# One sum tensor instead of two in a macaron block of two MoE layers and attention

## What is computed

```python
x = x + 0.5 * ffn(layernorm(x), w_gate, w_shared_up, w_shared_down, w_up, w_down)
x = x + attention(layernorm(x), Wq, bq, Wk, bk, Wv, bv, Wo, bo)   # 16 query heads, 1 key/value head of 32
x = x + 0.5 * ffn(layernorm(x), ...)

def ffn(x, ...):                       # E = 64 experts, top 6, room for CAP = 256 rows in each
    y_s, g_s = split(x @ w_shared_up)
    shared = silu(g_s) * y_s @ w_shared_down
    scores = sigmoid(x @ w_gate)
    w, topk_idx = top6(scores)         # w divided by its sum
    # pos = place of a row in its expert's list; rows beyond CAP are dropped
    x_disp[e, pos] = x[row]
    g_r, v_r = split(x_disp @ w_up)    # 512 -> 2 x 64, per expert
    out_r = silu(g_r) * v_r @ w_down   # 64 -> 512
    routed[row] = sum over the row's experts of w * out_r[e, pos]
    return shared + routed
```

## Time and profile before

| | us |
|---|---|
| median of 3 runs (lowest, highest) | 3214.35 (3210.79, 3216.09) |
| span of the profiled execution | 3211.7 |
| route0 | 0 to 185 |
| experts0 | 185 to 617 |
| project | 617 to 820 |
| attention | 820 to 2544 |
| route1 | 2544 to 2714 |
| experts1 | 2714 to 3143.5 |
| combine | 3143.5 to 3211.7 |

### The profile page before, as it was taken

One profiled execution on the slowest core, in us unless ns is written; L12 is line 12 of the kernel. 1 busy time (PEld: TensorE's weight loads), 2 busy tenths in 40 slices (PEclk: granted clock), 3 DMA queues, 4 the chain that ended last, 5 costly groups with the idle time before them and its releaser, 6 DMA issues. The chain is left out here.

```text
span 3211.7 us, 44845 instructions
## 1 busy us (share of the span) xinstructions
PE 2799.2 (87%) x15264; PEld 1631.1 (51%) x15264; DVE 2037.6 (63%) x3922; ACT 1526.7 (48%) x2871; POOL 2216.7 (69%) x1430
## 2 busy tenths in 40 slices
PE   8967777398899999999999999999999876888870
PEld 4644444176555555555555555555554374555540
DVE  7833222267788788788787887887876294333334
ACT  5522222153566566566565665665656352222220
POOL 2248888562688788788787887887878423677770
PEclk9978888699999999999999999999999867999995
DMA  5679999894567677676776776776757364899998
GB/s 213 214 203 241 246 235 235 198 276 168 118 146 145 132 171 146 147 148 140 154 150 132 172 142 147 147 145 149 155 121 153 104 212 154 202 233 234 243 184 321
DMA packets 216987, 575.78 MB, mean 179 GB/s; under 512 B 33980, under 2 KB 35004, under 8 KB 192824
## 3 DMA queue, kind: packets, MB, share of 16 engines
q0 software_dynamic: 87296, 343.98, 53.2%
q1 hardware_dynamic: 125240, 220.55, 21.1%
q10 hardware_dynamic: 4224, 8.39, 0.7%
HBM read 230.94 MB, written 155.24 MB: 120 GB/s over the span
## 5 line engine op out<-in xcount | busy, mean ns | idle before, releaser
L1915 DVE TENSOR_REDUCE attention_mx<-attention_pM 128x1 f32<-128x512 f32 x1984 | 1209.4, 682 | 180.1 <-PE attention_pM L1774 175.7
L1719 ACT ACTIVATE attention_prob<-attention_pS 128x512 f32<-128x512 f32 x2048 | 1035.9, 628 | 528.7 <-PE attention_pS L1761 528.5
L1660 POOL TENSOR_TENSOR attention_pair<-attention_prob 128x1024 f32<-128x1024 f32 x380 | 947.4, 2499 | 189.4 <-ACT attention_prob L1719 174.7
L1761 PE MATMUL attention_pS<-attention_qT,prep_kT 128*128 128x512 f32 x2048 | 832.7, 413 | 2.5 <-ACT attention_prob L1719 1.5
L1774 PE MATMUL attention_pM<-prep_kT,attention_qT 96*128 96x512 f32 x1984 | 804.4, 408 | 0.0
L1761 PEld LDWEIGHTS attention_pS<-attention_qT,prep_kT 128*128 128x128 f32 x2048 | 387.3, 189 | 289.4 <-issue 160.0
L1799 PE MATMUL attention_pO<-attention_prob,attention_v 128*32 128x512 f32 x4096 | 492.5, 598 | 0.0
L768 POOL DMA_INDIRECT sum<-experts_res,c_table x256 | 404.0, 1578 | 123.2 <-issue 78.0
L1774 PEld LDWEIGHTS attention_pM<-prep_kT,attention_qT 96*128 96x128 f32 x1984 | 374.7, 190 | 142.2 <-DVE attention_mx L1915 56.8
L752 POOL DMA_INDIRECT experts_rows<-xn_rows,c_table x256 | 250.7, 979 | 103.8 <-issue 71.3
L797 PE MATMUL experts_pT<-c_ident,experts_rows 128*128 128x128 f32 x1024 | 169.5, 306 | 120.2 <-issue 47.9
(11 more groups left out here) (181 smaller groups left out, 3141.3 us busy)
## 6 DMA issues: line engine op xcount, KB each, us to landing
prep_acc<-attention_pair POOLq DMA_DIRECT2D x96, 1024.0 KB, 7.7
attention_acc<-attention_pair POOLq DMA_DIRECT2D x90, 1024.0 KB, 7.6
attention_qT<-q_parts SPq DMA_DIRECT2D x96, 256.0 KB
xn_rows<-route_xn SPq DMA_DIRECT2D x16, 1152.0 KB, 6.7
experts_wup<-in_L_ffn_w_up_dram SPq DMA_DIRECT2D x64, 256.0 KB
q_parts<-prep_acc SPq DMA_DIRECT2D x64, 256.0 KB, 4.3
ahead_wup<-in_L_ffn_w_up_dram SPq DMA_DIRECT2D x64, 256.0 KB, 9.1
combine_got<-sum SPq DMA_DIRECT2D x16, 1024.0 KB
```

The source lines that it names most:

```text
L1660: pool.tensor_tensor(to[:, part], prob[2 * n % PROBS][:, part], prob[(2 * n + 1) % PROBS][:, part], ALU.add).then_inc(s_pair, 1)
L1719: act.activation(prob[t % PROBS][:, h * QT:(h + 1) * QT], pS[:, at, :], ACT.Exp).then_inc(s_ex, 1)
L1761: pe.matmul(pS[:, at, :], kT[:, key:key + P], qT[g][:, h, :], start=True, stop=True).then_inc(s_sc, 1)
L1915: dve.tensor_reduce(mx[:, unit, part:part + 1], pM[:, r % RING, :], X, ALU.max).then_inc(s_mr, 1)
```

## The change

Each FFN has one sum tensor. In the experts stage, both experts of a pair add onto it. The order on POOL becomes: two gathers, the two adds of a pair's first expert, two gathers, the two adds of its second one. The first two wait until the second expert's adds of the pair before have landed, the second two until the first two have. In `route0` POOL adds x to the shared rows (`with_x`), after `rsqrt` of the turn two ahead and ahead of the next `places`, and SP stores the result as the sum's start; x stays in its buffer until then, so that its ring has four buffers there, and a load waits for `with_x` too. `route1` writes no zeros, and the semaphore of the stored rows is split by ring slot. `project` loads one tensor, without `add_sums` and `bring`; `combine` loads one tensor and makes one addition a turn.

```diff
 def route(...)
-    XB, RING, HOTS = 3, 4, 2 * TURN
+    XB, RING, HOTS = 4 if kept is None else 3, 4, 2 * TURN
...
                 def load(i):
                     if i >= XB:
                         sp.wait_ge(s_xn, A + (i - XB + 1) * TURN)
+                        if kept is None:
+                            sp.wait_ge(s_sx, A + (i - XB + 1) * TURN)
...
-                    if copy_x:
-                        own_rows = slice(i * QT, (i + 1) * QT)
-                        sp.dma_start(sums[0][own_rows, :].rearrange("(p n) c -> p (n c)", p=P),
-                                     x_d[own_rows, :].rearrange("(p n) c -> p (n c)", p=P)).then_inc(s_nil, 16)
                     if kept is None:
-                        sp.wait_ge(s_sh, A + (i + 1) * TURN)
-                        sp.dma_start(half_view[i, :, :, :], sh[i % 2][:, :, :]).then_inc(s_so[i % 2], 16)
-                    else:
-                        sp.dma_start(half_view[i, :, :, :], zero[:, 0:C].unsqueeze(1).to_broadcast([P, TURN, C])
-                                     ).then_inc(s_so[i % 2], 16)
+                        sp.wait_ge(s_sx, A + (i + 1) * TURN)
+                        sp.dma_start(sum_view[i, :, :, :], sh[i % 2][:, :, :]).then_inc(s_so[i % 2], 16)
...
+                def with_x(i, j):
+                    pool.wait_ge(s_sh, A + i * TURN + (j + 1))
+                    pool.sem_inc(k["pool_on"], 1)
+                    pool.tensor_tensor(sh[i % 2][:, j, :], sh[i % 2][:, j, :], xt[i % XB][:, j, :], ALU.add
+                                       ).then_inc(s_sx, 1)
+
                 for i in range(-2, NTURN + 1):
...
+                    if comes(i) and kept is None:
+                        for j in range(TURN):
+                            with_x(i, j)
...
 def experts(...)
-                def add_rows(e):
-                    for a in range(2):
...
-                        if e > 0:
-                            pool.wait_ge(s_add[a], e * (16 * HALVES))
...
-                                sums[a], bass.IndirectOffsetOnAxis(ap=k["table"][:, 2 * e + a, h:h + 1], axis=0),
...
+                def add_rows(e, a):
...
+                    if a == 0 and e > 0:
+                        pool.wait_ge(s_add[1], e * (16 * HALVES))
+                        pool.sem_inc(k["pool_on"], 1)
+                    if a == 1:
+                        pool.wait_ge(s_add[0], (e + 1) * (16 * HALVES))
+                        pool.sem_inc(k["pool_on"], 1)
+                    for h in range(HALVES):
+                        pool.indirect_dma_start(
+                            sums, bass.IndirectOffsetOnAxis(ap=k["table"][:, 2 * e + a, h:h + 1], axis=0),
+                            res[e % 2][:, a, h, :], None, compute_op=ALU.add
+                            ).then_inc(s_add[a], 16)
...
                 for e in range(PAIRS + AHEAD):
-                    if there(e):
-                        gather(e)
-                    if there(e - AHEAD):
-                        add_rows(e - AHEAD)
+                    for a in range(2):
+                        if there(e):
+                            gather(e, a)
+                        if there(e - AHEAD):
+                            add_rows(e - AHEAD, a)
...
 def combine(...)
                 for i in range(NTURN):
-                    for a in range(2):
-                        src = sums[a][i * (TURN * P):(i + 1) * (TURN * P), :].rearrange("(t p) c -> p t c", p=P)
-                        sp.dma_start(got[i][a][:, :, :], src).then_inc(s_g[a][i], 16)
+                    src = sums[i * (TURN * P):(i + 1) * (TURN * P), :].rearrange("(t p) c -> p t c", p=P)
+                    sp.dma_start(got[i][:, :, :], src).then_inc(s_g[i], 16)
...
 def project(...)
-                    sp.dma_start(got[i % RING][:, :, :], turn_view[0][i, :, :, :]).then_inc(s_g[i % RING], 16)
-                    if i < ADDED:
-                        sp.dma_start(other[i][:, :, :], turn_view[1][i, :, :, :]).then_inc(s_g[i % RING], 16)
+                    sp.dma_start(got[i % RING][:, :, :], turn_view[i, :, :, :]).then_inc(s_g[i % RING], 16)
...
-                    if (s + 6) % TURN == 0 and ADDED <= i < NTURN:
-                        bring(i)
...
-                    if s < ADDED * TURN:
-                        add_sums(s, s // TURN, s % TURN)
```

More of the change, by code:

```diff
@@ L113, in setup, with route @@
     return k
-def route(nc, tag, k, wts, x_d, xn_d, sums, copy_x, prep=None, later=None, kept=None, first=None):
+def route(nc, tag, k, wts, x_d, xn_d, sums, prep=None, later=None, kept=None, first=None):
     w_gate, w_su, w_sd = wts
-    XB, RING, HOTS = 3, 4, 2 * TURN
+    XB, RING, HOTS = 4 if kept is None else 3, 4, 2 * TURN
     QT = TURN * P
@@ L204, in route @@
         s_wd = m.sem("wd")
-        s_row = m.sem("row")
+        s_row = m.sems("row", RING)
         s_pos = m.sem("pos")
@@ L773, in _ @@
-                for e in range(PAIRS + AHEAD):
-                    if there(e):
-                        gather(e)
-                    if there(e - AHEAD):
-                        add_rows(e - AHEAD)
+                    for h in range(HALVES):
+                        pool.indirect_dma_start(
+                            rows[e % RING][:, a * HALVES + h, :], None, xn_d,
+                            bass.IndirectOffsetOnAxis(ap=k["table"][:, 2 * e + a, h:h + 1], axis=0)
+                        ).then_inc(s_g[a][e % RING], 16)
@@ L778, in _ @@
+                for e in range(PAIRS + AHEAD):
+                    for a in range(2):
+                        if there(e):
+                            gather(e, a)
+                        if there(e - AHEAD):
+                            add_rows(e - AHEAD, a)
                 for a in range(2):
@@ L976, in combine @@
         m = Memory(nc, ctx, tag)
-        got = [[m.sb(f"got{i}{a}", [P, TURN, C]) for a in range(2)] for i in range(NTURN)]
-        s_g = [m.sems(f"g{a}", NTURN) for a in range(2)]
-        s_two = m.sem("two")
+        got = [m.sb(f"got{i}", [P, TURN, C]) for i in range(NTURN)]
+        s_g = m.sems("g", NTURN)
         s_add = m.sem("add")
@@ L1114, in project @@
         got = [m.sb(f"got{b}", [P, TURN, C]) for b in range(RING)]
-        other = [m.sb(f"other{b}", [P, TURN, C]) for b in range(ADDED)]
         stats = m.sb("stats", [P, TURN, 6])
@@ L1157, in x_tile @@
             return got[t // TURN % RING][:, t % TURN, :]
-        def loads(i):
-            return i // RING + (2 if i % RING < ADDED else 1)
-        def brought(i):
-            return i // RING + (0 if i % RING < ADDED else 1)
         def first_blocks(s, half):
@@ L1174, in project @@
         SLOTS = NT + PARTS
-        turn_view = [part[0:N, :].rearrange("(i t p) c -> i p t c", t=TURN, p=P) for part in sums]
+        turn_view = sums[0:N, :].rearrange("(i t p) c -> i p t c", t=TURN, p=P)
         with nc.Block() as block:
@@ L1361, in _ @@
             def _(dve):
-                begin(dve, s_add, s_st, s_ve, s_vb, s_xl, s_lo, s_kl, ahead["reduced"])
-                def add_sums(t, i, j):
-                    dve.wait_ge(s_g[i % RING], A + 16 * loads(i))
-                    dve.tensor_tensor(x_tile(t), x_tile(t), other[i][:, j, :], ALU.add).then_inc(s_add, 1)
+                begin(dve, s_st, s_ve, s_vb, s_xl, s_lo, s_kl, ahead["reduced"])
                 def moments(t, i, j):
-                    if i < ADDED:
-                        dve.wait_ge(s_add, A + t + 1)
-                    else:
-                        dve.wait_ge(s_on[i % RING], 16 * brought(i))
+                    dve.wait_ge(s_g[i % RING], A + 16 * (i // RING + 1))
                     dve.sem_inc(k["dve_on"], 1)
@@ L2026, in program @@
         xn_d = nc.dram_tensor("xn_rows", (N + P, ROW), F32).ap()
-        sums = [[nc.dram_tensor(f"sum{n}{a}", (N + P, C), F32).ap() for a in range(2)] for n in range(2)]
+        sums = [nc.dram_tensor(f"sum{n}", (N + P, C), F32).ap() for n in range(2)]
         xb_d = nc.dram_tensor("x_rows", (N, C), F32).ap()
```

82 lines of the change are left out of this document (32 added, 50 removed).

## The result

The changed kernel takes 3489.23 us (3485.84 to 3492.42) against 3214.99 of the kernel before: a ratio of 1.0858, 95% interval 1.0843 to 1.0873. The profiled execution has a span of 3484.0 us, 272.3 more than before.

What follows compares the result with a forecast made beforehand. POOL's issuing of indirect DMAs was taken to bound the experts stages. The span 3211.7 + 262.9 - 20.9 - 13 + 12 = 3452.7, with the median 2.65 above it, gave 3455 us; range 3365 to 3580, chance 0.80.

Steps and rivals of the forecast that it cites:

- The chain: Experts stages: every half-pair waits for the landing of the one before, link 8.2 us; together +262.9 us.
- The first rival: Experts stages: two gathers cover landing and restart, so only the savings are left, 3192 us; chance 0.05.
- the short link of 6.81: Experts stages: one sum's adds meet emptier queues, link 6.81 us, time 3280 us; chance 0.05.
- the loaded link of 9.9: Experts stages: gathers issued just ahead share the queue and weights' loads go on, total some 3670 us; chance 0.08.
- The fourth rival: First route: the lock between DVE and POOL costs its full 43.5 us, beside the forecast's chain, 3486 us; chance 0.02.
- The first route: First route: POOL's 32 additions hold up DVE, PE hides part; +12 us, between ends of 0 and 43.5.
- The combine: Combine: one of three passes of 8.39 MB goes, at 0.402 MB per us; -20.9 us, or -15.
- The projection: Projection's start: earlier first load, additions and the wait disappear; -13 us, between -8 and -16.
- The second route: Second route: loses the store of zeros, which nothing waits for; left at 0.
- The signs named for the forecast: POOL idle 1 to 3 us per half-pair, 16 to 17 per pair; ACT, DVE not awaiting adds; combine near 47 us.
- the signs named for being wrong: POOL's adds still idle by "issue", or idle times under 1 or over 4 us; first route longer than 200 us.

## Why the prediction was right, point by point

**The chain.** The step that decided, that two gathers cannot cover a landing and POOL has to wait for every half-pair, held in all 126 links; that the cost is that wait and neither the tensor nor the order was shown by the three runs on two tensors. The first rival (the gathers cover the landing) fell: the shortest link of all is 7.58. So did the short link of 6.81; the loaded link of 9.9 is reached by single links, up to 10.23, but not by the mean. The fourth rival, the lock in the first route at its full price, would have given 3486, which is nearer to the measured 3489 than the forecast is. That is chance: the experts stages took 30 us more than the forecast and the route 20.2 and not 43.5, so the number alone could not have told the two apart, and the stages do.

**Its size** is where the forecast fell 34 us short. The link was taken as 8.2 and is 8.44 in the mean (8.47 and 8.41 in the two stages), which is 126 x 0.24 = 30 us: +293.3 in place of +262.9. Two parts of the term were too small. The issue of two adds was taken from the end of the stage of before, 3.42; it is that at the end of the stage here as well (adds of 1.55 us), but among gathers an add takes 1.62 and 1.59, and the pair is 3.51 in the mean of all. The wait was taken as 4.78, half way between an emptiest and a mean landing, since the queues would be emptier; it is 4.93, though the DMA share of the first stage fell from 0.97 to 0.76. The link of the end, 7.88, is what "emptier" would have given, and the weights' loads alone make 0.33 us of what the mean lies above it, as the run without them shows.

The 34 us are these 30, 5 of the first route, and 2.6 by which the median lies further above the profiled span than before (5.2 in place of 2.65), less some 4 in the other terms.

**The first route** cost 17.0 up to the first add, 20.2 up to the first gather, and not 12, inside the bounds of 0 and 43.5. The mechanism was the named one, DVE held up by POOL's additions, shown by the run with a copy. Both sizes in it were too small. POOL's additions took 51.4 us and not the 43.5 of the projection's, and DVE's operations grew by 26.2 us where half of 43.5, 21.8, was taken: the four groups above by 27.8 and others by 5.7, less the 7.3 that `route_ve` no longer loses. And PE, which was to hide about half, hid some 6 us of it (26.2 less 20.2), since it waits for just these operations (`route_mask`).

**The combine** gave 24.0 and not 20.9. The 25.2 MB that the prediction lets it read are what it moves: by its 16 loads of 1 MB it reads 16.8 MB, and it stores 8.4. The whole stage moves 369 GB/s with two tensors and with one, so the time of the bytes that go is 8.39 MB / 0.369 = 22.7; taking the first 5.5 us out as fixed was the mistake, and 1.1 us more came between the last add and the first load.

**The projection** gave 12.4 where 13 was taken, but the terms do not come out as well as the sum, and that is luck. The third tile's statistics come 4.8 us earlier after the first load, which are the second load and the additions, as taken. The stall between the third and the fourth is 5.6 us and not 7.5, since a tile takes 3.5 there without it and not 1.6. The 2 us that are left came behind these tiles, where the prediction had nothing; what they are was not looked for. The runs with later loads show that the stall did not need one tensor. **The second route** and the attention moved by less than 1 us each, as said.

The signs named for the forecast are there, except one. POOL waits 2.66 us in the mean, in 92 of the 126 cases between 1 and 3; a pair of experts takes 16.9 us, the combine 45.3, and the projection's first product comes 12.7 us earlier after the first load. But ACT and DVE go on waiting for adds, and much longer than before (433.4 and 627.8 us, since they wait for the same landings). That sentence of the prediction was wrong. It has no cost, since POOL is the one that is late. One of the signs named for being wrong is there as well: the first route lasts 205 us, longer than 200. It goes back to the size of the route's term and leaves the chain as it is.

## What to carry to other kernels

A read-modify-write onto memory with an order to keep is a chain, and its price is the number of links times issue plus landing plus restart, minus the work that can be put between; count what lies between two dependent ones before one of two targets is taken away, for here the second target was what hid the landing. What one target saves elsewhere (here 36 us of loading) is to be held against all links (here 126, each longer by 2.3 us). An addition moved to an idle engine is not free when a busy one's operations last longer beside it: look which of these a critical engine waits for.

## What the runs showed of the hardware

An accumulating indirect DMA of 128 rows of 2 KB, two in a row, lets its waiting engine go 4.2 to 4.8 us after the end of their issue when no gathers and no loads of weights are left; with rows of 1 KB it is 3.0 us. The Trainium skill, "DMA: Bandwidth & Descriptors", section "Anatomy of one DMA — SWDGE (gpsimd) path", has a fixed 2.0 us and 436 GB/s, by which half of the bytes would save an estimated 0.3 us of one add, or 0.6 of two that move one behind the other, and not 1.5: for accumulating onto scattered rows in this kernel the part that goes with the bytes is larger than that.

Gathers issued behind such an add do not delay its landing measurably (8.48 us from half to half with none between, 8.44 with two), while loads of weights by another queue do (0.33 us per link).

DVE operations of 0.29 us with two inputs last 1.05 and 1.24 in the mean of a stage in which POOL makes its additions. The Trainium skill, "SBUF — State Buffer", section "Who interferes with whom", says that DVE with two inputs in SBUF and a reading GpSimd shut each other out; these rows agree.
